# Small TensorE products padded with zeros to the full 128 rows and columns, in an audio tower on one core

## The chip, the cores and the metric

The kernel runs on one core of a Trainium2 chip. The metric is the device time of one execution in microseconds (us), lower is better. A core has five engines that run side by side, each through its own list of instructions in order: TensorE (PE in the profile, its weight loads apart as PEld), VectorE (DVE), ScalarE (ACT), GpSimd (POOL) and SyncE (SP, which here only issues DMAs). They wait for one another with semaphores.

TensorE multiplies a stationary operand (rows x columns, loaded by a LDWEIGHTS) with a moving operand that streams past it. The profile writes a product's form as `rows*columns` of the stationary operand, then `rows x columns` of the moving one: `16*128 16x121` has 16 rows of contraction, 128 stationary columns (rows of the result) and 121 moving columns. Each fp32 product leaves two MATMUL records, so x8 in a row of the trace is four products.

## The reference, cut to what matters

The input is 32 sequences of 80000 samples. Each is cut into 626 frames of 128 samples (zero-padded) and goes through a transform and four layers with residual sums, each behind a layer norm:

```python
h = frames(x) @ dct.T                                   # 626 tokens x 128
# 1: Mamba2, forwards and backwards: xBC = silu(conv4(u @ Win.T)), B and C are 16 columns each of it;
#    h_t = h_{t-1} * dA_t + dt_t * B_t x_t ;  y_t = C_t . h_t + D x_t ; gate, norm, projection
h = h + attn0(norm(h))
# 2: mixture of 8 experts, top 2: gelu(u @ w1 + b1) @ w2 + b2, weighed and summed
h = h + ffn0(norm(h))
# 3: attention over a window of 8 following tokens, per channel
h = h + attn1(norm(h))
# 4: gelu(u @ ip.T), top 64 of 512; gelu(. @ pw.T), top 128 of 256; softmax weights;
#    agg = weights @ process_values (64 columns); gelu(agg @ ow.T), top 64 of 512; @ op
h = h + ffn1(norm(h))
```

## The kernel before

One sequence is one block of work, and its four layers are four stages (`*_stage1` to `*_stage4`). Five tiles of 128 tokens make a sequence. The stages are pipelined over the sequences: in one iteration of the loop `Fori`, stage 1 works on sequence b, stage 2 on b-1, stage 3 on b-2 and stage 4 on b-3. With 32 sequences there are 35 iterations, the first three and the last three with fewer stages (written out), 29 full ones in between. In this text an iteration is cut at the first write of `h2` by VectorE (L1158) in one sequence and the next.

Each stage is written as a generator for each engine, and a string of digits (`PE_ORDER`, `ACT_ORDER`, `DVE_ORDER`, `POOL_ORDER`, `SP_ORDER`) says from which stage an engine takes its next piece. So each engine's order is fixed and mixes pieces of four stages; an engine that waits for one piece holds all pieces behind it.

What TensorE does, with the lines of the profile:

- Stage 1, projections (L566): 20 half units per sequence, each 4 products (the taps of the convolution) or 1 product (z) of 315 moving columns. Unit 0 of each direction makes B and C: its stationary operand has only `BC` = 48 columns (16 for B, a gap of 16, 16 for C), the result 48 rows. ScalarE applies silu and writes B to `Bw` and C to `Cs`, tiles of 16 rows.
- Stage 1, mixing: 12 chunks per sequence (6 chunks, 2 directions). For each, `mix(k)` makes the product C.B (L577, 16 rows of contraction, 121 moving columns) and two transposes of the inputs (L584); VectorE weighs the inputs (`Xw`, L1080) and the decays times C.B (`Mt`, L1083); `combine(k)` makes the skip products (L594) and four products of 64 stationary columns (L600); ScalarE copies the result (L863). Behind them stand the output products (L620) and row sums of 1 moving column (L628), for which VectorE waits at L1094.
- Stage 2, experts: MT = 17 tiles per sequence. `up(i)` has four products (L675), ScalarE applies gelu, and `down(i)` begins with the bias b2, added as a product of one row (a row of ones times b2, L684), then has four products (L686) and a transpose of a later tile (L663).
- Stage 4: for each of the 5 tiles transposes (L754), four products with 256 moving columns (L762), transposes (L772), the value product (L777, 64 stationary columns, so a result of 64 rows, copied to `aggT` by ScalarE, L992), the product with `owT` (L782, 64 rows of contraction, 512 moving columns), transposes (L791) and four products (L796), whose result VectorE adds at L1281.

VectorE's own work is above all the top-k selection of stage 4 (MAX8 and MATCH_REPLACE8, L1219, L1222, L1249, L1252), the scans of stage 1 (L1072) and the elementwise work of stage 3.

Of the kernel before, what the change touches and what calls it, by code (L numbers as in the profile page):

```python
# [13 lines left out]
P = 128  # L14
# [5 lines left out]
NS = 16  # L20
NH = 4
HD = 64
# [10 lines left out]
BC = 48  # L33
CW = 2 * P + BC
# [30 lines left out]
    ("ipT", NI), ("pwT", 4 * NP_), ("pv", 2 * HD), ("owT", NO), ("op", 4 * P),  # L65
# [72 lines left out]
def audio_tower(nc, NB, consts_d, setup_d, x_d, out_d, rows_d, experts_d, routed_d, answers_d):  # L138
    ctx = ExitStack()
    with ctx:  # L140
# [64 lines left out]
        Bw = [sb(f"Bw{d}", [NS, CH, P]) for d in range(2)]  # L205
        Cs = [sb(f"Cs{d}", [NS, CH, WIN]) for d in range(2)]
# [46 lines left out]
        aggT = sb("aggT", [HD, P])  # L253
# [23 lines left out]
        def weights_of(d, unit):  # L277

            if unit < 3:
                lo, n = ((2 * P, BC), (0, P), (P, P))[unit]  # L280
                return [(wconv[:, d, i, lo:lo + n], i) for i in range(TAPS)]
            z = c("wz").rearrange("p (d g n) -> p d g n", d=2, g=2)
            return [(z[:, d, unit - 3, :], TAPS - 1)]
# [10 lines left out]
        def b2_of(i):  # L294
            return expert[i % WR][0:1, 8 * P + KB:EC]
# [204 lines left out]
        def _(pool):  # L500
# [10 lines left out]
            for d in range(2):  # L511
                nc.gpsimd.memset(Bw[d][:, :, WIN:P], 0.0)
# [9 lines left out]
        def pe_stage1(pe, b):  # L522
# [27 lines left out]
            for n in range(HALF_UNITS):  # L550
                yield
                d, unit, half = n // 10, n % 10 // 2, n % 2
                yield
                if n == 2:
                    pe.wait_ge(G["dt_arg"].s, G["dt_arg"](b, 1))
                if n >= 3:
                    pe.wait_ge(G["proj_sb"].s, G["proj_sb"](b, n - 2))
                if n == DA_UNIT:

                    pe.wait_ge(G["dt_act"].s, G["dt_act"](b, 3))  # L560
                    at = 512 * (n % 3) + DA_AT
                    nc.tensor.transpose(pS[:, at:at + WIN], dtA_wide[:], ident[0:WIN, 0:WIN]).then_inc(G["dA_ps"].s, 1)
                blocks = weights_of(d, unit)
                rows = BC if unit == 0 else P
                for j, (wt, i) in enumerate(blocks):
                    last = nc.tensor.matmul(pS[0:rows, 512 * (n % 3):512 * (n % 3) + HQ], wt, tap(d, i, half * HQ, HQ),  # L566
                                            start=(j == 0), stop=(j == len(blocks) - 1))
                last.then_inc(G["proj_ps"].s, 1)
# [62 lines left out]
        def pe_stage2(pe, b):  # L631
# [47 lines left out]
            def down(i):  # L679
# [4 lines left out]
                nc.tensor.matmul(at, c("ones", 1), b2_of(i), start=True, stop=False)  # L684
# [53 lines left out]
        def pe_stage4(pe, b):  # L738
# [25 lines left out]
            for t in range(TILES):  # L764
# [11 lines left out]
                for j in range(2):  # L776
                    last = nc.tensor.matmul(pD[0:HD, 512:512 + P], c("pv")[:, j * HD:(j + 1) * HD], selT[:, j * P:(j + 1) * P],  # L777
# [4 lines left out]
                nc.tensor.matmul(pD[:, 0:NO], aggT[:], c("owT", HD), start=True, stop=True).then_inc(G["a3_ps"].s, 1)  # L782
# [30 lines left out]
        def act_stage1(act, b):  # L813
# [23 lines left out]
            for n in range(HALF_UNITS):  # L837
# [9 lines left out]
                if unit == 0:  # L847
                    nc.scalar.activation(Bw[d][:, half * CH // 2:(half + 1) * CH // 2, NS:WIN], px[0:NS].rearrange("p (c t) -> p c t", c=CH // 2),
                                         ACT.Silu, bias=cb[0:NS, d, 2:3])
                    last = nc.scalar.activation(Cs[d][:, half * CH // 2:(half + 1) * CH // 2, 0:Q], px[32:32 + NS].rearrange("p (c t) -> p c t", c=CH // 2),  # L850
# [108 lines left out]
        def act_stage4(act, b):  # L959
# [26 lines left out]
            for t in range(TILES):  # L986
# [5 lines left out]
                nc.scalar.copy(aggT[:], pD[0:HD, 512:512 + P]).then_inc(G["agg_sb"].s, 1)  # L992
# [9 lines left out]
        def _(act):  # L1002
# [4 lines left out]
            for d in range(2):  # L1007
                for ch in range(CH):
                    nc.scalar.copy(Bw[d][:, ch, 0:NS], ident[0:NS, 0:NS])
                    last = nc.scalar.copy(Cs[d][:, ch, Q:WIN], ident[0:NS, 0:NS])  # L1010
# [344 lines left out]
def laid_out(a):  # L1355
# [12 lines left out]
    def bc(x):  # L1368

        gap = np.zeros(x.shape[:-1] + (NS,), x.dtype)  # L1370
        return np.concatenate([x[..., 0:272], gap, x[..., 272:288]], -1)
# [20 lines left out]
    o["pv"] = a["L1_ffn_process_values"].reshape(2, P, HD).transpose(1, 0, 2)  # L1392
# [49 lines left out]
```

## Time and profile before

| | |
|---|---|
| device time, 3 runs | 8329.64 us median, 8313.04 to 8416.84 |
| profiled execution, span | 8631.7 us (what lies around the span is not shown; its time is at least this) |
| PE busy | 6340.7 us, 73% |
| DVE busy | 6951.3 us, 81% |
| ACT busy | 3240.6 us, 38% |
| POOL busy | 3053.8 us, 35% |
| mean granted TensorE clock | 0.752 of 2.4 GHz |

The busy time of an engine is the time in which it has an instruction at work. The clock granted to TensorE has two levels here, 1.00 (2.4 GHz) and 0.50 (1.2 GHz); 0.752 is their mean over the span. The profiled execution is 302 us longer than the median of the runs.

### The profile page before, as it was taken

The page shows a single profiled execution, that of the slowest core. Times are in us where ns is not written, and L with a number is a line of the kernel's source. Part 1 is how long each engine was busy: PE and PEld are TensorE (multiplying, and loading weights), DVE is VectorE, ACT ScalarE, POOL GpSimd, SP SyncE. Part 2 cuts the span into 40 slices and gives each one's busy share as a digit, 9 for nine tenths or more (in the row PEclk, how much of TensorE's full clock was granted, in tenths as well). Part 3 has the DMA queues.
Part 4 walks back from the last instruction along what each step waited for, and adds up shares of the span by engine and source line. Part 5 has one row for each costly group of instructions (what it writes and reads, how often), then busy time and mean ns, then how long its engine had stood idle before and what let it go on. Part 6 is the DMA issues. An engine that isn't in the chain of part 4 may idle for free.

```text
span 8631.7 us, 109592 instructions
## 1 busy us (share of the span) xinstructions
PE 6340.7 (73%) x31240; PEld 4768.2 (55%) x31240; DVE 6951.3 (81%) x22124; ACT 3240.6 (38%) x7204; POOL 3053.8 (35%) x3190
## 2 busy tenths in 40 slices
PE   6777778777777777777777777777777777777633
PEld 4555556555565555555555555555555555555422
DVE  2377978878888878889887979788879787889787
ACT  2343334433444433444443334433334433344311
POOL 2343433333333334333333433333333333333320
PEclk8887777776787767788776778777778777788655
DMA  2321222211222212222221222212222211222200
GB/s 68 103 79 52 61 79 75 69 55 54 69 79 75 65 47 67 69 80 76 74 63 50 61 78 77 72 57 59 59 79 76 71 58 55 62 80 76 62 6 3
DMA packets 342763, 561.43 MB, mean 65 GB/s; under 512 B 33728, under 2 KB 261792, under 8 KB 341664
## 3 DMA queue, kind: packets, MB, share of 16 engines
q10 hardware_dynamic: 152576, 357.68, 13.4%
q1 hardware_dynamic: 168992, 153.36, 6.8%
q0 software_dynamic: 20480, 41.98, 1.6%
q8 instruction: 311, 5.10, 0.3%
q14 instruction: 404, 3.31, 0.1%
HBM read 484.15 MB, written 68.74 MB: 64 GB/s over the span
## 4 chain that ended last, share of the span: by engine, by line
DVE 52%; PE 20%; issue 14%; DMA 4%; POOL 4%; ACT 3%; another core or an unknown queue 1%; ACTq 1%; SPq 1%; DVEq 0%; POOLq 0%
DVE m L1219 10%; DVE work L1252 7%; DVE work L1222 6%; DVE sorted L1249 6%; DVE a L1222 3%; PE pS L566 3%; DMA rows<-routed_rows 3%; DVE lg L1174 2%; DVE ab L1072 2%; PE pM L675 2%; PE pS L628 2%; PE pD L762 2%; PE pM L686 1%; POOL u L388 1%; DVE Mt L1083 1%
## 5 line engine op out<-in xcount | busy, mean ns | idle before, releaser
L1219 DVE MAX8 m<-work 128x8 f32<-128x512 f32 x1792 | 1144.6, 680 | 1.0
L1222 DVE MATCH_REPLACE8 work<-m,work 128x512 f32<-128x512 f32 x1536 | 1025.9, 675 | 0.0
L566 PE MATMUL pS<-u_fm,wconv_s 128*128 128x315 f32 (+1 forms) x3072 | 966.6, 470 | 0.2
L675 PE MATMUL pM<-turned,expert 128*128 128x128 f32 x4352 | 739.8, 323 | 244.2 <-ACT turned L921 243.2
L675 PEld LDWEIGHTS pM<-turned,expert 128*128 128x128 f32 x4352 | 660.9, 229 | 346.2 <-issue 328.6
L686 PE MATMUL pM<-expert,hid 128*128 128x128 f32 x4352 | 798.3, 340 | 0.0
L908 ACT ACTIVATE hid<-pM,expert 128x128 f32<-128x128 f32 x2176 | 619.4, 367 | 385.6 <-PE pM L675 383.8
L460 POOL TENSOR_TENSOR lg<-lg,red 128x640 f32<-128x640 f32 x256 | 388.2, 1553 | 996.5 <-DVE red L1180 996.5
L566 PEld LDWEIGHTS pS<-u_fm,wconv_s 128*128 128x128 f32 (+1 forms) x3072 | 526.6, 179 | 387.2 <-issue 154.7
L686 PEld LDWEIGHTS pM<-expert,hid 128*128 128x128 f32 x4352 | 674.6, 237 | 81.9 <-issue 35.1
L1252 DVE MATCH_REPLACE8 work<-sorted,work 128x128 f32<-128x128 f32 x2240 | 591.5, 276 | 0.0
L1219 DVE MAX8 m<-a 128x8 f32<-128x512 f32 x768 | 504.4, 677 | 71.7 <-issue 70.2
L1249 DVE MAX8 sorted<-work 128x8 f32<-128x128 f32 x2560 | 541.7, 279 | 1.1
L411 POOL TENSOR_TENSOR yg<-xs,zs 128x525 f32<-128x525 f32 (+1 forms) x256 | 198.0, 806 | 962.7 <-ACT xs L863 951.6
L999 ACT COPY selT<-pD 128x512 f32<-128x512 f32 x160 | 93.6, 585 | 1169.8 <-PE pD L791 1008.2
L1072 DVE TENSOR_TENSOR_SCAN ab<-ab,cst 121x488 f32<-121x488 f32 x384 | 489.8, 1282 | 36.7 <-DMA ab<-decay_rows 36.7
L489 POOL TENSOR_TENSOR lg<-lg 128x640 f32<-128x640 f32 x224 | 362.6, 1642 | 440.3 <-DVE lg L1185 435.3
L466 POOL TENSOR_TENSOR red<-lg 128x640 f32<-128x640 f32 x128 | 197.8, 1582 | 748.0 <-ACT lg L951 748.0
L921 ACT COPY turned<-pM 128x256 f32<-128x256 f32 (+1 forms) x544 | 196.7, 362 | 699.6 <-issue 356.2
L1080 DVE TENSOR_TENSOR Xw<-pS,dts 121x256 f32<-121x256 f32 x384 | 157.9, 411 | 367.2 <-PE pS L584 362.6
L600 PE MATMUL pS<-Mt,Xw 121*64 121x121 f32 x3072 | 311.9, 336 | 163.0 <-DVE Mt L1083 163.0
L796 PE MATMUL pD<-cst,selT 128*128 128x128 f32 x1280 | 294.4, 401 | 185.7 <-ACT selT L999 130.8
(242 smaller groups left out, 14472.6 us busy)
## 6 DMA issues: line engine op xcount, KB each, us to landing
expert<-in_experts ACTq DMA_DIRECT2D x544, 578.0 KB
ab<-decay_rows SPq DMA_DIRECT2D x384, 230.7 KB
rows<-routed_rows SPq DMA_DIRECT2D x128, 256.0 KB, 4.8
answer_rows<-turned ACTq DMA_DIRECT2D x256, 128.0 KB, 3.9
x_sb<-in_x SPq DMA_DIRECT2D x32, 256.0 KB
out<-hk SPq DMA_DIRECT2D x32, 256.0 KB
routed_rows<-un,slot POOLq DMA_INDIRECT x320
rows<-answer_rows,slot POOLq DMA_INDIRECT x320
```

The lines of the kernel that those rows point to most:

```text
L460: last = nc.gpsimd.tensor_tensor(lg[:, w, :], lg[:, w, :], red[:, 0, :], ALU.subtract)
L489: last = nc.gpsimd.tensor_tensor(lg[:, w, :], lg[:, w, :], lg[:, w + n, :], ALU.add)
L566: last = nc.tensor.matmul(pS[0:rows, 512 * (n % 3):512 * (n % 3) + HQ], wt, tap(d, i, half * HQ, HQ), start=(j == 0), stop=(j == len(block ...
L600: last = nc.tensor.matmul(pS[r * HD:(r + 1) * HD, B2 + g * WIN:B2 + (g + 1) * WIN], Xw[d][:, hh, :], Mt[d][:, hh, :], start=False, stop=(g ...
L675: last = nc.tensor.matmul(pM[:, bank(i) + j * P:bank(i) + (j + 1) * P], w1_of(i, j), turned[:, (i + 2) % 4, 1, :], start=True, stop=True)
L686: last = nc.tensor.matmul(at, hid[:, i % 2, j, :], w2_of(i, j), start=False, stop=(j == KB - 1))
L908: last = nc.scalar.activation(hid[:, i % 2, j, :], pM[:, at:at + P], ACT.Gelu, bias=b1_of(i, j))
L1072: nc.vector.tensor_tensor_scan(decays, decays, c("scan_src", WIN), 0.0, ALU.mult, ALU.add).then_inc(G["scanned"].s, 1)
L1219: link(nc.vector.max(m8[:, i, :], now[i]), len(tiles) - 1)
L1222: link(nc.vector.match_replace(work[i], m8[:, i, :], now[i], GONE), len(tiles) - 1)
L1249: link(nc.vector.max(top[:, 8 * r:8 * r + 8], left), 2 * n - 1)
L1252: link(nc.vector.match_replace(left, top[:, 8 * r:8 * r + 8], left, GONE), 2 * n - 1)
```

## The change

The products with few rows or columns are given zeros up to 128, and work on whole tiles:

- B and C projection: the stationary operand of unit 0 grows from 48 to 128 columns (`CW` from 304 to 384; the added columns of `wconv` and `convw` are zeros), the result from 48 to 128 rows. ScalarE still reads the same 32 rows of it.
- C.B: `Bw` and `Cs` grow from 16 to 128 rows, cleared once in the setup; the product has 128 rows of contraction.
- Expert bias: the row of ones becomes the whole 128x128 tile of ones, and b2 is read with all 128 rows, of which 127 are zeros already.
- Value product: `pv` gets 64 columns of zeros; the result has 128 rows, `aggT` 128 rows, and the product with `owT` 128 rows of contraction.

The number of instructions in the iterations and their order on every engine stay as they are. The four products of 64 columns at L600 stay as they are.

```diff
-BC = 48
-CW = 2 * P + BC
+CW = 3 * P
...
-    ("ipT", NI), ("pwT", 4 * NP_), ("pv", 2 * HD), ("owT", NO), ("op", 4 * P),
+    ("ipT", NI), ("pwT", 4 * NP_), ("pv", 2 * P), ("owT", NO), ("op", 4 * P),
...
-        Bw = [sb(f"Bw{d}", [NS, CH, P]) for d in range(2)]
-        Cs = [sb(f"Cs{d}", [NS, CH, WIN]) for d in range(2)]
+        Bw = [sb(f"Bw{d}", [P, CH, P]) for d in range(2)]
+        Cs = [sb(f"Cs{d}", [P, CH, WIN]) for d in range(2)]
...
-        aggT = sb("aggT", [HD, P])
+        aggT = sb("aggT", [P, P])
...
-                lo, n = ((2 * P, BC), (0, P), (P, P))[unit]
+                lo, n = ((2 * P, P), (0, P), (P, P))[unit]
...
-            return expert[i % WR][0:1, 8 * P + KB:EC]
+            return expert[i % WR][:, 8 * P + KB:EC]
...
-                nc.gpsimd.memset(Bw[d][:, :, WIN:P], 0.0)
+                nc.gpsimd.memset(Bw[d][:], 0.0)
+                nc.gpsimd.memset(Cs[d][:], 0.0)
...
-                rows = BC if unit == 0 else P
                 for j, (wt, i) in enumerate(blocks):
-                    last = nc.tensor.matmul(pS[0:rows, 512 * (n % 3):512 * (n % 3) + HQ], wt, tap(d, i, half * HQ, HQ),
+                    last = nc.tensor.matmul(pS[:, 512 * (n % 3):512 * (n % 3) + HQ], wt, tap(d, i, half * HQ, HQ),
...
-                nc.tensor.matmul(at, c("ones", 1), b2_of(i), start=True, stop=False)
+                nc.tensor.matmul(at, c("ones"), b2_of(i), start=True, stop=False)
...
-                    last = nc.tensor.matmul(pD[0:HD, 512:512 + P], c("pv")[:, j * HD:(j + 1) * HD], selT[:, j * P:(j + 1) * P],
+                    last = nc.tensor.matmul(pD[:, 512:512 + P], c("pv")[:, j * P:(j + 1) * P], selT[:, j * P:(j + 1) * P],
...
-                nc.tensor.matmul(pD[:, 0:NO], aggT[:], c("owT", HD), start=True, stop=True).then_inc(G["a3_ps"].s, 1)
+                nc.tensor.matmul(pD[:, 0:NO], aggT[:], c("owT"), start=True, stop=True).then_inc(G["a3_ps"].s, 1)
...
-                nc.scalar.copy(aggT[:], pD[0:HD, 512:512 + P]).then_inc(G["agg_sb"].s, 1)
+                nc.scalar.copy(aggT[:], pD[:, 512:512 + P]).then_inc(G["agg_sb"].s, 1)
```

ScalarE's writes to `Bw` and `Cs` name the first 16 rows now, and the host lays the zeros into `wconv`, `convw` and `pv`.

## Rows read from the trace of the kernel before

**Rows 1.** The page: span, chain of waits by engine, granted clock in 40 slices

```profile
span 8631.7 us, 109592 instructions
...
PEclk8887777776787767788776778777778777788655
...
DVE 52%; PE 20%; issue 14%; DMA 4%; POOL 4%; ACT 3%; another core or an unknown queue 1%; ACTq 1%; SPq 1%; DVEq 0%; POOLq 0%
...
```

**Rows 2.** Stretches: ramp-up and steady part, a row each

```profile
...
core 0: us, PE busy (x) PEld busy (x) DVE busy (x) ACT busy (x) POOL busy (x), PEclk, DMA share, GB/s
0.00:508.10 508.10, 362.86 (x2021) 277.30 (x2021) 152.55 (x408) 155.92 (x374) 169.36 (x207) 0.83 0.28 85
508.10:8017.80 7509.70, 5709.30 (x28304) 4310.36 (x28304) 6287.61 (x20039) 2954.26 (x6525) 2764.19 (x2871) 0.76 0.23 67
...
```

**Rows 3.** Stretches: the 13 long iterations, longest one and sum

```profile
...
5417.40:5690.40 273.00, 209.34 (x976) 157.97 (x976) 216.70 (x691) 101.95 (x225) 95.46 (x99) 0.72 0.21 64
...
sum 3495.50, PE 2689.25 PEld 2026.89 DVE 2824.20 ACT 1323.91 POOL 1239.46; mean PE 206.87 PEld 155.91 DVE 217.25 ACT 101.84 POOL 95.34
```

**Rows 4.** Stretches: the 16 short iterations, shortest one and sum

```profile
...
774.50:1019.10 244.60, 184.40 (x976) 138.67 (x976) 216.18 (x691) 101.75 (x225) 96.09 (x99) 0.81 0.24 71
...
sum 4014.20, PE 3020.05 PEld 2283.47 DVE 3463.40 ACT 1630.36 POOL 1524.72; mean PE 188.75 PEld 142.72 DVE 216.46 ACT 101.90 POOL 95.30
```

**Rows 5.** VectorE's waits in the long iteration 4381.2 to 4652.7

```profile
...
DVE Xw L1080 <- PE pS L584: 17.5, 5, 7.4
...
DVE vare L1094 <- PE pS L628: 5.5, 1, 5.5
DVE hk L1281 <- PE pD L796: 3.8, 2, 2.3
...
```

**Rows 6.** VectorE's waits in the short iteration 4132.7 to 4381.2

```profile
...
DVE Xw L1080 <- PE pS L584: 3.3, 2, 2.2
...
```

**Rows 7.** Stretches: 12 cold and busy ones, inside long iterations

```profile
...
4531.90:4600.10 68.20, 66.75 (x257) 47.60 (x257) 48.60 (x98) 17.28 (x55) 15.23 (x11) 0.50 0.23 65
...
sum 518.90, PE 508.88 PEld 365.65 DVE 342.54 ACT 126.66 POOL 124.32; mean PE 42.41 PEld 30.47 DVE 28.55 ACT 10.55 POOL 10.36
```

**Rows 8.** Stretches: a cold one without small products, and what follows it

```profile
...
4138.10:4142.70 4.60, 4.60 (x7) 1.63 (x6) 2.81 (x21) 1.56 (x3) 1.27 (x2) 0.50 0.00 2
4142.70:4152.90 10.20, 7.68 (x40) 4.75 (x39) 9.35 (x25) 5.18 (x12) 5.73 (x13) 1.00 0.00 0
...
```

**Rows 9.** TensorE in order of time, clock at 0.50, no idle time

```profile
...
4539.04 0.79 PE L684 MATMUL pM<-expert,cst 1*128 1x128 f32 x2
4539.76 2.08 PE L686 MATMUL pM<-expert,hid 128*128 128x128 f32 x8
4541.63 0.42 PE L663 MATMUL pM<-cst,rows 128*128 128x128 f32 x1
...
4543.82 2.07 PE L782 MATMUL pD<-cst,aggT 64*128 64x512 f32 x2
4545.83 0.78 PE L577 MATMUL pS<-Cs,Bw 16*128 16x121 f32 x2
4546.53 0.69 PE L584 MATMUL pS<-cst,xs 128*128 128x128 f32 x2
...
```

**Rows 10.** TensorE in order of time, clock at 1.00

```profile
...
4044.09 0.48 PE L684 MATMUL pM<-expert,cst 1*128 1x128 f32 x2
4044.50 1.16 PE L686 MATMUL pM<-expert,hid 128*128 128x128 f32 x8
4045.50 0.27 PE L663 MATMUL pM<-cst,rows 128*128 128x128 f32 x1
...
```

**Rows 11.** Weight loads of the projections, the two forms apart

```profile
...
L566 PEld LDWEIGHTS pS<-u_fm,wconv_s 128*128 128x128 f32 x2048 | 373.2, 190 | 162.2 <-issue 22.6 <-ACT Cs L850 9.8 <-DVE dtA L1063 5.0
...
L566 PEld LDWEIGHTS pS<-u_fm,wconv_s 128*48 128x48 f32 x1024 | 153.4, 157 | 225.0 <-issue 132.2 <-ACT zs L856 22.8
...
```

**Rows 12.** GpSimd in order of time, its longest memset of the setup

```profile
...
3.74 2.56 POOL L515 MEMSET xs<- 128x2968 f32 x1
...
```

More of the change, by code:

```diff
@@ L847, in act_stage1 @@
                 if unit == 0:
-                    nc.scalar.activation(Bw[d][:, half * CH // 2:(half + 1) * CH // 2, NS:WIN], px[0:NS].rearrange("p (c t) -> p c t", c=CH // 2),
+                    nc.scalar.activation(Bw[d][0:NS, half * CH // 2:(half + 1) * CH // 2, NS:WIN], px[0:NS].rearrange("p (c t) -> p c t", c=CH // 2),
                                          ACT.Silu, bias=cb[0:NS, d, 2:3])
-                    last = nc.scalar.activation(Cs[d][:, half * CH // 2:(half + 1) * CH // 2, 0:Q], px[32:32 + NS].rearrange("p (c t) -> p c t", c=CH // 2),
+                    last = nc.scalar.activation(Cs[d][0:NS, half * CH // 2:(half + 1) * CH // 2, 0:Q], px[32:32 + NS].rearrange("p (c t) -> p c t", c=CH // 2),
                                                 ACT.Silu, bias=cb[32:32 + NS, d, 2:3])
@@ L1008, in _ @@
                 for ch in range(CH):
-                    nc.scalar.copy(Bw[d][:, ch, 0:NS], ident[0:NS, 0:NS])
-                    last = nc.scalar.copy(Cs[d][:, ch, Q:WIN], ident[0:NS, 0:NS])
+                    nc.scalar.copy(Bw[d][0:NS, ch, 0:NS], ident[0:NS, 0:NS])
+                    last = nc.scalar.copy(Cs[d][0:NS, ch, Q:WIN], ident[0:NS, 0:NS])
             last.then_inc(a_exp, 1)
@@ L1370, in bc @@
         gap = np.zeros(x.shape[:-1] + (NS,), x.dtype)
-        return np.concatenate([x[..., 0:272], gap, x[..., 272:288]], -1)
+        return np.concatenate([x[..., 0:272], gap, x[..., 272:288], np.zeros(x.shape[:-1] + (P - 3 * NS,), x.dtype)], -1)
     o["wconv"] = np.concatenate([bc(x[256:544].T) for x in w], 1)
@@ L1391, in laid_out @@
     o["pwT"] = a["L1_ffn_process_input_weights"].T.reshape(4, P, NP_).transpose(1, 0, 2)
-    o["pv"] = a["L1_ffn_process_values"].reshape(2, P, HD).transpose(1, 0, 2)
+    pv = a["L1_ffn_process_values"].reshape(2, P, HD).transpose(1, 0, 2)
+    o["pv"] = np.concatenate([pv, np.zeros_like(pv)], -1)
     o["owT"] = a["L1_ffn_output_input_weights"].T
```

## The prediction, made before the changed kernel ran

> **What bounds the kernel now.** I read the page first. The chain of waits is 52% VectorE and 20% TensorE, and the granted clock moves between 0.5 and 0.8 or more in the slices [rows 1]. In the 7509.7 us of the 29 full iterations VectorE is busy 6287.6 us (84%) and TensorE 5709.3 us (76%) at a mean clock of 0.76; in the first 508.1 us TensorE is busy 362.9 us and VectorE 152.6 us [rows 2]. So VectorE bounds the steady part, and TensorE counts where VectorE waits for it. VectorE's 1222 us of idle time there is all that a faster TensorE could touch.
>
> Next I cut the steady part into its iterations, a row each. The work is the same in all (976 TensorE records), yet there are two kinds: 13 long ones, together 3495.5 us, 268.9 us each, up to 273.0 [rows 3], and 16 short ones, together 4014.2 us, 250.9 us each, down to 244.6 [rows 4]. VectorE's busy time is equal (217.3 and 216.5 us). TensorE's is 206.9 against 188.8 us, and its clock 0.70 to 0.74 against 0.77 to 0.81. The difference of 18.0 us is the clock's.
>
> VectorE's waits say where it lands. In a long iteration it waits 17.5 us at L1080 for the transposes of the mixing (L584), 5.5 us at L1094 and 3.8 us at L1281 [rows 5]; in a short one 3.3 us at L1080 [rows 6].
>
> Then I looked at TensorE just ahead of those waits. Twelve of the 13 long iterations hold one stretch of 34 to 68 us in which TensorE is busy nearly throughout and the clock stays at 0.50: 508.9 us busy of 518.9, VectorE busy 342.5 [rows 7]. The longest is 66.75 busy of 68.2 us. No short iteration has one over 17 us. In order of time such a stretch is the mixture of experts, chunks of the mixing and stage 4, with a bias product (L684, 1 row), a C.B product (L577, 16 rows) or an `owT` product (L782, 64 rows) every 2 to 3 us [rows 9]. Elsewhere a cold piece made of full products alone, 4.60 us of 4.60 busy, is followed by 10.2 us at 1.00 [rows 8]. So being busy doesn't bring the clock up in the first kind of stretch and does in the second, and what stands in the first and not in the second are products with few rows and the 64-column products of L600. The Trainium skill ("TensorE: Matmul & The Clock Gate", "What's actually happening") says that the gate goes by how busy TensorE has been; the 68 us stretch doesn't agree, unless few rows count for less, of which the page says nothing.
>
> **What the change does, part by part.**
>
> *Bias product, 17 per iteration.* Cold, it takes 0.72 us from its start to that of L686, while the four full products of the same width behind it take 1.87 us, 0.47 each [rows 9]. Warm it is 0.41 us against 1.00/4 = 0.25 [rows 10]. A padded bias product is in form exactly one of L686. It saves 0.25 us cold, 0.16 warm: 4.3 or 2.7 us per iteration. The Trainium skill says otherwise: in the same page, "Why this matters for your kernels", a product of 32 rows takes as long as one of 128, by which the saving would be 0. The rows show one of 1 row taking longer. The page "TensorEngine Tiling (Array Packing)", "Key Properties", gives a reason that agrees: a change of tiling mode drains TensorE.
>
> *C.B product, 12 per iteration.* 0.70 us cold [rows 9] against 0.47 for 128 moving columns: 0.23 saved, 2.8 us per iteration; warm, by the bias product's 0.16, 1.9 us. Its tiles are cleared once and their first 16 rows alone are rewritten, so nothing is added inside the loop.
>
> *`owT` product, 5 per iteration.* 2.01 us cold for 512 moving columns [rows 9], against 4 x 0.47 = 1.87: 0.14 saved, 0.7 us per iteration. ScalarE's copy to `aggT` has 128 rows in place of 64 and the same 128 elements per row; I take 0.
>
> *Value product, 10 per iteration, and B/C projection, 16 per iteration (four half units of 4).* These gain columns, not rows. The nearest row for a gain is the bias product's 0.25 us, for a loss the weight load: 157 ns for 48 columns against 190 ns for 128 [rows 11], 33 ns per record, two records per product. If it lay bare it would cost 32 x 0.033 = 1.1 us per iteration. The products of 315 columns beside it are far longer (by the 0.47 us for 128 columns cold, over 1 us), so they cover it. I take 0, the row of loads being nearer, and keep -2.5 and +1.1 us for the range.
>
> *Sum on TensorE.* 4.3 + 2.8 + 0.7 = 7.8 us per iteration cold, about 5 warm, some 6 in a short iteration.
>
> *What of it reaches the end.* In a short iteration VectorE waits 3.3 us for the mixing; with 6 us less ahead of it I take 2.5 of the 3.3, since part of TensorE's run begins only when VectorE has released it. 29 x 2.5 = 72 us. The bounds are 0, if the run always starts at VectorE's own release, and 3.3 x 29 = 96.
>
> *The clock.* If the small products are what holds the clock at 0.50, the cold stretches end within a few us, and the long iterations become short ones. All 13 would give 13 x 18.0 = 234 us. From the other side, 508.9 us of cold busy time run at twice the clock gives 254; the two agree. I take 11 of 13, since L600 keeps its 64 columns and some iterations will still fall badly: 198 us. The bounds are 0 and 234.
>
> *Ramp-up.* In 508.1 us TensorE is ahead of VectorE; about two iterations of small products, 2 x 6 = 12 us.
>
> *Setup.* Four memsets of 768 or 726 columns replace two tiny ones: 2988 columns at 2.56/2968 = 0.86 ns [rows 12] are 2.6 us, on the path, as TensorE, ScalarE and the zeroing DMA wait for `pool_setup`. With the larger constants +4 us. Nothing covers it, and it is paid once.
>
> The sum against the profiled execution is 198 + 72 + 12 - 4 = 278 us: its span would go from 8631.7 to about 8354, 3.2% less.
>
> **From the span to the median.** The median is 302 us under that span, more than the 234 us of all 13 long iterations. Either the profiler costs time, or the runs have fewer long iterations; their spread of 104 us is 6 of them. If they have few, there is less to win. I take two thirds of the clock's term, 130 us: 8330 - 130 - 72 - 12 + 4 = **8120 us**.
>
> **Rivals.**
>
> *A: only the switches are saved.* The runs have hardly a long iteration, or the padded zeros don't lift the clock. By the skill's rule that the gate goes by busy time it would be so too. What is left is 72 + 12 - 4 = 80: 8250 us, 8200 to 8300. For it speaks the median, which is near an execution of short iterations alone (8631.7 - 234 = 8398, and lower); against it the 12 stretches.
>
> *B: it doesn't do what it says, for time.* A product of 128 rows of zeros costs what one of 1 row does, and the 0.72 us were the wait for hid or the bank: about 8335. Against it: C.B, with other tiles and other waits, shows the same 0.70.
>
> *C: slower.* TensorE gets through its work sooner, so it idles longer before each release by VectorE; the clock falls in these gaps, and each run then begins at 0.50. The place is the mixing and L620 to L628, and it shows in the short iterations becoming long: 16 x 18.0 = 288 us, less the 80: 8540 us. It decides against the change once more than 5 of the 16 turn (80/18 = 4.4) with none of the long ones cured. For it speaks that TensorE idles 62 us in a short iteration already; against it that the short iterations, which idle no less, are the warm ones.
>
> **How the numbers follow.** Forecast 0.62, A 0.27, B 0.05, C 0.06. The low end is both terms whole and half of the value product's bound (2.5 x 32 = 80), 8330 - 234 - 96 - 40 = 7960; the high end reaches through A to 8270. Two per cent, about what a measurement of this kernel can tell from no change, is 8163. The forecast case lies under it but for a few hundredths, and A's lower end hardly reaches it: faster 0.61, same 0.33, slower 0.06.
>
> **What the profile after would show.** Right: a mean clock of 0.80 or more; no cold, busy stretch over 20 us; nearly all iterations at 245 to 252 us; the bias product at 0.47 or 0.25 us; VectorE's wait at L1080 (L1079 there) at 4 us or less in nearly every iteration. VectorE's waits at L1094 and L1281 stay, as the products ahead of them were full before. Wrong: long iterations still about a dozen (the clock isn't held by the small products), or the switch time still at the padded products.

## The result, and the profile after

| | before | after |
|---|---|---|
| device time, median | 8339.6 us (8313.04 to 8416.84, 4 runs) | 8142.81 us (8130.81 to 8145.41, 4 runs) |
| ratio, 95% interval | | 0.9727 (0.9667 to 0.9787) |
| profiled execution, time and span | 8631.7 us span | 8142.98 us, span 8141.2 us |

The kernel is 2.7% faster by the ratio, an estimate of its own with its interval, and 2.4% by the quotient of the two medians (0.9764). Its runs also lie within 14.6 us of one another, those of before within 104 us. Ratios are taken over undisturbed runs alone, while a median may stand over all of them, so the two can differ by some tenths of a per cent below too.

The page of the changed kernel, its lines that answer to [rows 1], with the busy time of the engines ahead of them:

```profile
span 8141.2 us, 109594 instructions
...
PE 5529.4 (68%) x31240; PEld 4441.6 (55%) x31240; DVE 6959.1 (85%) x22124; ACT 3232.6 (40%) x7204; POOL 3040.7 (37%) x3192
...
PEclk8887788878788888788877788878788878778755
...
DVE 67%; PE 9%; issue 8%; DMA 5%; POOL 5%; ACT 3%; ACTq 2%; SPq 1%; DVEq 0%; POOLq 0%
```

The mean clock went from 0.752 to 0.800, and VectorE's share of the chain from 52 to 67%: VectorE is still at work 6959 us, and waits less. Next the stretches of the changed kernel, cut as in [rows 2 to 4]: the ramp-up, the longest iteration, then the sum of all 29 full iterations.

```profile
...
core 0: us, PE busy (x) PEld busy (x) DVE busy (x) ACT busy (x) POOL busy (x), PEclk, DMA share, GB/s
0.00:491.40 491.40, 332.92 (x2021) 273.49 (x2021) 154.37 (x408) 155.51 (x374) 173.59 (x209) 0.85 0.29 89
...
3646.80:3891.80 245.00, 173.48 (x976) 139.44 (x976) 216.80 (x692) 101.79 (x226) 94.68 (x99) 0.80 0.25 71
```

```profile
...
sum 7045.80, PE 4961.00 PEld 4004.98 DVE 6293.62 ACT 2946.70 POOL 2746.90; mean PE 171.07 PEld 138.10 DVE 217.02 ACT 101.61 POOL 94.72
```

There is one kind of iteration left: 240.9 to 245.0 us, 243.0 in the mean, with TensorE busy 171.1 us in each against 206.9 and 188.8 [rows 3, 4]. No stretch of 17 us or more is busy throughout at 0.50 any longer. Before, there were twelve of 34 us and more by [rows 7], and a thirteenth that the prediction overlooked, in the one long iteration that it took for an exception (1019.1 to 1281.9). So every long iteration has one:

```profile
...
1169.70:1214.10 44.40, 43.00 (x168) 30.93 (x168) 26.09 (x44) 11.84 (x38) 13.29 (x8) 0.50 0.28 83
```

The waits of VectorE over the whole execution (total, times, longest):

```profile
...
DVE work L1240 <- ACT a L970: 239.9, 30, 8.7
...
DVE Xw L1079 <- PE pS L583: 158.5, 103, 20.6
...
DVE hk L1280 <- PE pD L795: 57.8, 35, 4.0
DVE vare L1093 <- PE pS L627: 50.5, 3, 17.8
```

The wait for the mixing (L1079, L1080 before) is 158.5 us in 103 places, ramp-up and end included. The 29 full iterations alone, 491.4 to 7537.2, have less than half of it:

```profile
...
DVE Xw L1079 <- PE pS L583: 64.8, 87, 2.6
```

That is 2.2 us per iteration, 3.8 in the worst; in one long iteration of before it was 17.5 us, in a short one 3.3 [rows 5, 6]. TensorE in order of time, first at 1.00, then at 0.50, to be read beside [rows 10] and [rows 9]:

```profile
...
2031.92 0.39 PE L683 MATMUL pM<-expert,cst 128*128 128x128 f32 x2
2032.15 1.06 PE L685 MATMUL pM<-expert,hid 128*128 128x128 f32 x8
2033.04 0.27 PE L662 MATMUL pM<-cst,rows 128*128 128x128 f32 x1
```

```profile
...
2069.41 0.64 PE L683 MATMUL pM<-expert,cst 128*128 128x128 f32 x2
2069.84 1.92 PE L685 MATMUL pM<-expert,hid 128*128 128x128 f32 x8
2071.55 0.42 PE L662 MATMUL pM<-cst,rows 128*128 128x128 f32 x1
```

From start to start the bias product (L683) takes 2032.15 - 2031.92 = 0.23 us warm, where it was 0.41, and 2069.84 - 2069.41 = 0.43 us cold, where it was 0.72. A product of L685 takes (2033.04 - 2032.15)/4 = 0.22 warm and (2071.55 - 2069.84)/4 = 0.43 cold. The padded product is a full one, and costs what a full one costs. The four products of L685 became quicker too, though nothing in them was changed: 0.89 us warm against 1.00 [rows 10], 1.71 cold against 1.87 [rows 9]. From the bias product to the transpose of L662 it is 1.12 us against 1.41 warm and 2.14 against 2.59 cold. So one tile saves 0.29 and 0.45 us, where the prediction had 0.16 and 0.25.

**A difference that isn't the change's.** The profiled execution of before had a span of 8631.7 us, 302 over the median beside it. The runs below were made on three chips, and the unchanged kernel takes 8330.58 us on one of them, 8617.28 and 8620.74 on the two others. By its level that trace comes from a chip like the latter two, the times and the trace of after from one like the former; the waits of ScalarE shown further down say the same. So each kernel below is compared with the unchanged one on its own chip, and "the quicker chip" and "the slower chip" are said where it matters. Of e1, e2, e3 and e5 below the whole interval lies under 1, but the ratio is less than 2% away from it.

### The profile page after: what moved, and what is told of

The parts are those of the page before. It is cut to its first block, busy times and chain, and to the rows that moved or that the text cites. A ratio compares the mean times of both kernels' runs of the same rounds, so it can differ in the third digit from the quotient of the medians.

```text
span 8141.2 us, 109594 instructions
## 1 busy us (share of the span) xinstructions
PE 5529.4 (68%) x31240; PEld 4441.6 (55%) x31240; DVE 6959.1 (85%) x22124; ACT 3232.6 (40%) x7204; POOL 3040.7 (37%) x3192
## 3 DMA queue, kind: packets, MB, share of 16 engines
q10 hardware_dynamic: 152576, 357.68, 14.2%
## 4 chain that ended last, share of the span: by engine, by line
DVE 67%; PE 9%; issue 8%; DMA 5%; POOL 5%; ACT 3%; ACTq 2%; SPq 1%; DVEq 0%; POOLq 0%
DVE m L1218 15%; DVE work L1221 9%; DVE work L1251 7%; DVE sorted L1248 6%; DVE a L1221 4%; DVE ab L1071 3%; DMA rows<-routed_rows 3%; DVE lg L1173 2%; PE pS L565 2%; PE pD L761 2%; DVE Mt L1082 2%; DMA decay_rows<-dAT 2%; POOL u L387 2%; DVE stats L1030 2%; DVE red L1188 2%
## 5 line engine op out<-in xcount | busy, mean ns | idle before, releaser
L565 PE MATMUL pS<-u_fm,wconv_s 128*128 128x315 f32 x3072 | 929.0, 457 | 6.1 <-ACT Cs L849 5.8
L674 PE MATMUL pM<-turned,expert 128*128 128x128 f32 x4352 | 655.2, 297 | 331.7 <-ACT turned L920 327.4
L674 PEld LDWEIGHTS pM<-turned,expert 128*128 128x128 f32 x4352 | 586.0, 206 | 423.6 <-issue 359.9
L565 PEld LDWEIGHTS pS<-u_fm,wconv_s 128*128 128x128 f32 x3072 | 614.2, 205 | 256.3 <-issue 52.8
L685 PE MATMUL pM<-expert,hid 128*128 128x128 f32 x4352 | 672.9, 306 | 0.0
L685 PEld LDWEIGHTS pM<-expert,hid 128*128 128x128 f32 x4352 | 631.6, 223 | 0.0
L599 PE MATMUL pS<-Mt,Xw 121*64 121x121 f32 x3072 | 294.2, 321 | 488.7 <-DVE Mt L1082 486.4
L599 PEld LDWEIGHTS pS<-Mt,Xw 121*64 121x64 f32 x3072 | 189.2, 160 | 585.7 <-DVE Mt L1082 532.9
L382 POOL TENSOR_TENSOR rstd<-vare,mhalf 128x5 f32<-128x5 f32 x160 | 187.1, 1170 | 624.8 <-DVE vare L1036 624.8
```

What stands on the lines that cost most here:

```text
L565: last = nc.tensor.matmul(pS[:, 512 * (n % 3):512 * (n % 3) + HQ], wt, tap(d, i, half * HQ, HQ), start=(j == 0), stop=(j == len(blocks) - 1))
L599: last = nc.tensor.matmul(pS[r * HD:(r + 1) * HD, B2 + g * WIN:B2 + (g + 1) * WIN], Xw[d][:, hh, :], Mt[d][:, hh, :], start=False, stop=(g ...
L674: last = nc.tensor.matmul(pM[:, bank(i) + j * P:bank(i) + (j + 1) * P], w1_of(i, j), turned[:, (i + 2) % 4, 1, :], start=True, stop=True)
L685: last = nc.tensor.matmul(at, hid[:, i % 2, j, :], w2_of(i, j), start=False, stop=(j == KB - 1))
```

## The experiments

### One part of the change at a time, on the quicker chip

The unchanged kernel took 8330.58 us there (median of 19, 8235.92 to 8726.48).

`e1_bias_only`: the expert bias alone is padded.

```diff
-            return expert[i % WR][0:1, 8 * P + KB:EC]
+            return expert[i % WR][:, 8 * P + KB:EC]
...
-                nc.tensor.matmul(at, c("ones", 1), b2_of(i), start=True, stop=False)
+                nc.tensor.matmul(at, c("ones"), b2_of(i), start=True, stop=False)
```

> The kernel before with the bias product alone padded to 128 rows. Clock theory (products with few rows hold TensorE's clock at 0.50 though TensorE is busy): the bias stands in every cold stretch, so most of them end early; time 8180 to 8240 us, mean clock 0.77 or more, hardly an iteration over 262 us. Switch theory (only the time of changing the tiling mode is saved, 0.16 to 0.25 us a product, little of it where VectorE waits): 8290 to 8320 us, and the long iterations as many as in the kernel before. In both, a bias product takes 0.47 us cold and 0.25 us warm.

Measured: 8176.82 us, ratio 0.9871 (0.9802 to 0.9939), a little under the range of the clock theory. No iteration is over 245.6 us. The padded product takes 0.22 us warm, where 0.25 was expected.

`e2_cb_only`: the C.B product alone, with 128 rows of contraction.

```diff
-        Bw = [sb(f"Bw{d}", [NS, CH, P]) for d in range(2)]
-        Cs = [sb(f"Cs{d}", [NS, CH, WIN]) for d in range(2)]
+        Bw = [sb(f"Bw{d}", [P, CH, P]) for d in range(2)]
+        Cs = [sb(f"Cs{d}", [P, CH, WIN]) for d in range(2)]
...
```

The rest of this edit clears both tiles in the setup and lets ScalarE write their first 16 rows.

> The kernel before with C.B alone padded from 16 to 128 rows. Clock theory: it cures part of the cold stretches, 8210 to 8280 us. Switch theory: its 12 products stand right ahead of the transposes for which VectorE waits, 0.16 to 0.23 us each, so at most 2.5 us an iteration, 8260 to 8320 us, with long iterations left. This one tells the two apart by the iterations of the profile more than by the time.

Measured: 8214.36 us, ratio 0.9896 (0.9861 to 0.9931); no iteration over 246.1 us.

`e3_value_only`: the value product gets its 64 columns of zeros and the product with `owT` its 128 rows.

```diff
-                    last = nc.tensor.matmul(pD[0:HD, 512:512 + P], c("pv")[:, j * HD:(j + 1) * HD], selT[:, j * P:(j + 1) * P],
+                    last = nc.tensor.matmul(pD[:, 512:512 + P], c("pv")[:, j * P:(j + 1) * P], selT[:, j * P:(j + 1) * P],
...
-                nc.tensor.matmul(pD[:, 0:NO], aggT[:], c("owT", HD), start=True, stop=True).then_inc(G["a3_ps"].s, 1)
+                nc.tensor.matmul(pD[:, 0:NO], aggT[:], c("owT"), start=True, stop=True).then_inc(G["a3_ps"].s, 1)
...
```

> The kernel before with the value product (64 to 128 columns) and the product with owT (64 to 128 rows) alone padded. Clock theory: the owT product is the widest of the small ones (512 moving columns, 2.0 us cold), so fewer or shorter cold stretches, 8230 to 8300 us. Switch theory: 5 x 0.14 us an iteration, 8310 to 8340 us, the same as before.

Measured: 8177.55 us, ratio 0.9872 (0.9803 to 0.9941), more than either theory had said; no iteration over 246.3 us. Its 29 full iterations:

```profile
...
sum 7051.30, PE 5367.29 PEld 4100.40 DVE 6267.86 ACT 2951.10 POOL 2778.18; mean PE 185.08 PEld 141.39 DVE 216.13 ACT 101.76 POOL 95.80
```

They take 7051.3 us, the changed kernel's 7045.8, though TensorE is busy 185.1 us in each here and 171.1 there. So 14 us less work of TensorE per iteration are worth 0.2 us per iteration: in the full iterations the time of the small products themselves hardly reaches the end. In the ramp-up, where TensorE is ahead of VectorE, it does: the first 512.7 us of e3 are the first 491.4 of the changed kernel.

`e4_proj_only`: the B and C projection alone, 48 to 128 stationary columns.

```diff
-                lo, n = ((2 * P, BC), (0, P), (P, P))[unit]
+                lo, n = ((2 * P, P), (0, P), (P, P))[unit]
...
```

> The kernel before with the B and C projection alone padded from 48 to 128 columns. Both theories: no product has more rows, and the pitch of the 315-column products is set by the moving columns, so 8320 to 8360 us, the same as before. If the columns of the stationary operand counted for the clock too, it would be faster, 8200 to 8300 us. If the longer weight load (190 ns against 157) lay bare, slower by 1.1 us an iteration, 35 us.

Measured: 8311.18 us, ratio 0.9988 (0.994 to 1.0036), no change. Its profiled execution took 8338.82 us, as much as the 8339.6 of the kernel before. Its sums of the 11 long iterations and of the 18 short ones, then two of its cold and busy stretches, the longest one among them, and its wait for the mixing, over the whole execution and in the full iterations:

```profile
...
sum 2850.30, PE 2248.42 PEld 1722.97 DVE 2383.68 ACT 1119.40 POOL 1049.84; mean PE 204.40 PEld 156.63 DVE 216.70 ACT 101.76 POOL 95.44
```

```profile
...
sum 4374.00, PE 3334.41 PEld 2586.31 DVE 3890.12 ACT 1828.71 POOL 1720.30; mean PE 185.24 PEld 143.68 DVE 216.12 ACT 101.60 POOL 95.57
```

```profile
...
1394.20:1455.60 61.40, 59.84 (x233) 42.65 (x234) 41.24 (x77) 17.52 (x52) 15.88 (x9) 0.50 0.26 74
2629.80:2698.10 68.30, 66.81 (x257) 47.67 (x259) 48.70 (x98) 17.39 (x57) 15.35 (x11) 0.50 0.22 65
```

```profile
...
DVE Xw L1078 <- PE pS L582: 348.3, 111, 24.0
```

```profile
...
DVE Xw L1078 <- PE pS L582: 235.6, 94, 7.4
```

This kernel is in effect the kernel before, profiled on the quicker chip, which is what my working had lacked. Long iterations are 259.1 us, short ones 243.0, which is the changed kernel's mean. VectorE is equally busy in both, TensorE 204.4 against 185.2 us. The stretches at 0.50 are there in full length, 66.81 us busy of 68.3: eleven of 34 us or more, one in each long iteration and none in a short one. The wait for the mixing in a short iteration is 2.9 us in the mean, in a long one 16.7.

What follows from the four: three of the parts end the long iterations, each by itself: rows are added to 17, 12 or 5 products per iteration; the fourth, which pads columns of one product and no row of contraction, ends none.

### Rows, or the drain of the engine? On the slower chip

The unchanged kernel took 8617.28 us there (median of 7, 8598.0 to 8654.92). The question was whether the long iterations go because TensorE no longer stops between products of different form, or because more rows are at work.

`e7_bias_64_rows`: the bias product gets 64 rows, 63 of them zeros.

```diff
-            return expert[i % WR][0:1, 8 * P + KB:EC]
+            return expert[i % WR][0:64, 8 * P + KB:EC]
...
-                nc.tensor.matmul(at, c("ones", 1), b2_of(i), start=True, stop=False)
+                nc.tensor.matmul(at, c("ones", 64), b2_of(i), start=True, stop=False)
```

> The kernel before with the bias product at 64 rows in place of 1 (rows 1 to 63 of b2 are zeros). If the time lies in the switching and the product stays in a split mode at 64 rows, a product still takes 0.41 us warm and 0.72 cold. Clock theory with rows counting one by one: half of what 128 rows add, so most long iterations go, 8180 to 8260 us. Switch theory, or a clock that asks only for the full mode: as before, 8310 to 8350 us.

Measured: 8379.08 us, ratio 0.9717 (0.9682 to 0.9752). TensorE in order of time at 1.00, to be read beside [rows 10], the sum of the 29 iterations, and one of the longest stretches that are still cold and busy, 13.7 us:

```profile
...
2089.02 0.49 PE L684 MATMUL pM<-expert,cst 64*128 64x128 f32 x2
2089.43 1.16 PE L686 MATMUL pM<-expert,hid 128*128 128x128 f32 x8
2090.43 0.27 PE L663 MATMUL pM<-cst,rows 128*128 128x128 f32 x1
```

```profile
...
sum 7292.20, PE 5491.84 PEld 4160.27 DVE 6287.94 ACT 2956.61 POOL 2765.80; mean PE 189.37 PEld 143.46 DVE 216.83 ACT 101.95 POOL 95.37
```

```profile
...
4919.00:4932.70 13.70, 13.52 (x64) 10.57 (x65) 9.76 (x22) 5.36 (x20) 0.88 (x1) 0.50 0.46 118
```

The bias product takes 2089.43 - 2089.02 = 0.41 us, to the hundredth what it took with one row, the four products behind it 1.00 us as in [rows 10], and TensorE is busy 189.4 us per iteration, more than in a short one of before [rows 4]. So nothing was saved on the products, and yet no iteration is over 258.9 us and 2.8% of the time is gone. The products take the same time as before, so what ended the cold stretches isn't a change in TensorE's own timing. The Trainium skill ("TensorE: Matmul & The Clock Gate", "Why this matters for your kernels") has a product of 32 rows take as long as one of 128. This trace doesn't agree: 64 rows and 1 row cost the same here, 0.41 us, and 128 cost 0.18 us less.

`e6_zeros_added`: the bias product stays as it was, and a full product of a zeroed tile is added behind each one.

```diff
                 nc.tensor.matmul(at, c("ones", 1), b2_of(i), start=True, stop=False)
+                nc.tensor.matmul(at, c("ones"), none[:], start=False, stop=False)
...
```

> The kernel before, and behind each 1-row bias product one more full product of 128 rows that adds zeros (17 an iteration). All small products and their switches stay, and TensorE has 17 x 0.25 to 0.47 us more to do. Clock theory: more work and yet faster, since the clock comes up: 8190 to 8260 us, no long iterations. Switch theory: 4 to 8 us more for TensorE in each iteration, some of it where VectorE waits: 8340 to 8450 us.

Measured: 8461.67 us, ratio 0.9814 (0.9777 to 0.9852). TensorE in order of time at 0.50:

```profile
...
2161.05 0.79 PE L686 MATMUL pM<-expert,cst 1*128 1x128 f32 x2
2161.77 0.80 PE L687 MATMUL pM<-none,cst 128*128 128x128 f32 x2
2162.36 1.49 PE L689 MATMUL pM<-expert,hid 128*128 128x128 f32 x6
```

The one-row product keeps its 0.72 us, as in [rows 9], and a full one comes on top, 17 times per iteration. That one takes 2162.36 - 2161.77 = 0.59 us where a full one takes 0.43: the product behind a one-row product pays as well. The kernel has more work on TensorE and is 1.9% quicker. No iteration is over 260.6 us. Ten cold and busy stretches are left, but of 20.5 us each, 205 us together.

`e9_owt_rows_only`: only the product with `owT` gets 128 rows, 5 products per iteration; the value product keeps its 64 columns.

```diff
-        aggT = sb("aggT", [HD, P])
+        aggT = sb("aggT", [P, P])
...
+            nc.gpsimd.memset(aggT[:], 0.0)
...
-                nc.tensor.matmul(pD[:, 0:NO], aggT[:], c("owT", HD), start=True, stop=True).then_inc(G["a3_ps"].s, 1)
+                nc.tensor.matmul(pD[:, 0:NO], aggT[:], c("owT"), start=True, stop=True).then_inc(G["a3_ps"].s, 1)
...
-                nc.scalar.copy(aggT[:], pD[0:HD, 512:512 + P]).then_inc(G["agg_sb"].s, 1)
+                nc.scalar.copy(aggT[0:HD], pD[0:HD, 512:512 + P]).then_inc(G["agg_sb"].s, 1)
```

> The kernel before with five products an iteration changed: the product with owT has 128 rows of contraction in place of 64 (the added rows of aggT are cleared once); the value product keeps 64 columns. Clock theory: the rows are what counts, so this alone gives what padding value product and owT gave together, 8170 to 8190 us, with no iteration over 262 us. Switch theory: 5 x 0.14 us an iteration, 20 us at most, 8310 to 8340 us with long iterations left.

Measured: 8391.36 us, ratio 0.9741 (0.9697 to 0.9785); no iteration over 256.9 us. Its wait for the mixing:

```profile
...
DVE Xw L1081 <- PE pS L585: 212.8, 88, 28.5
```

Rows in five products per iteration end the long iterations; the value product's columns aren't needed for it.

`e5_all_but_bias`: the whole change without the bias.

```diff
-                nc.tensor.matmul(at, c("ones"), b2_of(i), start=True, stop=False)
+                nc.tensor.matmul(at, c("ones", 1), b2_of(i), start=True, stop=False)
...
```

> The changed kernel with the bias product back at 1 row. Clock theory: each part alone took the long iterations away, so taking one part back brings none: 8150 to 8180 us. Switch theory: the bias products are the most numerous, so half of the gain goes, 8220 to 8260 us.

Measured: 8495.16 us, ratio 0.9861 (0.9823 to 0.99). The long iterations are gone here too (250.9 to 256.9 us), but it is slower than e7 and e9 on the same chip, each of which does less. That was a miss, and asked for a look at the slower chip itself.

### What the slower chip does otherwise

These four ran on the third chip, the other one of the slower kind. The unchanged kernel took 8620.74 us there (median of 7, 8586.42 to 8679.01).

`e10_before_again` is the kernel before, and `e11_after_again` the changed one, both without any edit, to have the two traces from one chip.

> The kernel before, unchanged, for a trace from the same chip as the three runs beside it. The levels of two chips differed by some 280 us for it (8331 and 8617 us), while the share of its time that an edit saves was alike. Clock theory: 8 or more of the 29 full iterations are long (over 255 us) with a cold and busy stretch in each, and the short ones are as long as those of the changed kernel on this chip, within 3 us. Switch theory: all iterations are longer by some us, the short ones too.

> The changed kernel on the chip of the run before it. Both theories: 2 to 3.5% less than the kernel before. Clock theory: no cold and busy stretch over 25 us.

Measured: e10 8603.93 us with a span of 8602.1, so the profile adds nothing that shows. e11 8452.18 us, ratio 0.9787 (0.9727 to 0.9847), so whether it is 2% is open. e10 has ten iterations of 261.4 to 271.7 us, each with a cold and busy stretch of 34 us or more, and 19 of at most 258.9 us without one, 251.9 in the mean. e11 has no stretch of 17 us or more, and all its iterations lie between 245.4 and 257.0 us, but at 254.4 in the mean. So here the short iterations became 2.5 us longer. What was expected of e10 missed in its last part: its 13 iterations under 255 us are 249.8 in the mean, 4.6 under those of e11. The waits over the whole execution, of all engines, first e10, then e11:

```profile
...
DVE Xw L1080 <- PE pS L584: 339.4, 114, 29.1
...
ACT selT L999 <- remote: 149.1, 18, 9.4
...
DVE vare L1094 <- PE pS L628: 140.5, 26, 18.4
...
DVE hk L1281 <- PE pD L796: 112.3, 51, 4.1
```

```profile
...
ACT selT L998 <- remote: 231.8, 27, 9.7
...
DVE vare L1093 <- PE pS L627: 183.0, 30, 18.7
...
DVE Xw L1079 <- PE pS L583: 157.8, 103, 21.2
...
DVE hk L1280 <- PE pD L795: 141.9, 62, 4.1
```

The wait for the mixing falls by 339.4 - 157.8 = 182 us, as on the quicker chip (348.3 in e4, 158.5 in the changed kernel). But VectorE's waits at L1093 and L1280 (L1094 and L1281 before) grow by 183.0 + 141.9 - 140.5 - 112.3 = 72 us, and ScalarE's copy of `selT` waits 27 times, 8.6 us in the mean, for something for which the profile names no releaser (it calls it "remote"). VectorE's own waits at the two lines have some such entries too; with all entries counted they grow by 54 us. In the five traces from the quicker kind of chip (after, e1 to e4) the copy has no such wait. The trace of before has it, as e10 does:

```profile
...
ACT selT L999 <- remote: 151.7, 18, 9.3
...
```

TensorE around one of them, first e11, then the same place of the changed kernel on the quicker chip:

```profile
...
2991.37 0.66 PE L790 MATMUL pD<-cst,a 128*128 128x128 f32 x4 [0.78 <-issue]
...
2991.86 0.60 PE L722 MATMUL pA<-cst,kf 128*128 128x128 f32 x4
2998.20 2.08 PE L795 MATMUL pD<-cst,selT 128*128 128x128 f32 x8 [5.74 <-ACT selT L998]
3000.07 8.53 PE L627 MATMUL pS<-cst,zs 128*128 128x1 f32 x40
```

```profile
...
2893.99 0.60 PE L722 MATMUL pA<-cst,kf 128*128 128x128 f32 x4
2894.83 1.16 PE L795 MATMUL pD<-cst,selT 128*128 128x128 f32 x8 [0.24 <-ACT selT L998]
2895.83 4.73 PE L627 MATMUL pS<-cst,zs 128*128 128x1 f32 x40
```

The transposes of L790 that the copy reads had ended at 2992.03, but it began at 2997.56 only. TensorE idles 5.74 us for that copy, the granted clock falls to 0.50 in the gap, and the 40 row sums behind it (L627), for which VectorE waits, take 8.53 us in place of 4.73. In places like this one a part of the gain is given back on this chip.

`e12_small_added`: the changed kernel with a one-row product of zeros put back behind each padded bias product. If the stops of the engine counted, it would lose what the change won.

```diff
                 nc.tensor.matmul(at, c("ones"), b2_of(i), start=True, stop=False)
+                nc.tensor.matmul(at, c("ones", 1), none[0:1, :], start=False, stop=False)
...
```

> The changed kernel, and behind each padded bias product one more product of a single row that adds zeros: 17 switches into a split mode and back come back in each iteration, 0.41 us warm and 0.72 us cold each, 7 to 12 us of TensorE's time, and nothing is taken from the padded ones. Clock theory: the switches' time lies beside VectorE's work, so within 0.6% of the changed kernel, and no long iterations. Switch theory: most of the gain is lost, 1.5% or more over the changed kernel.

Measured: 8361.2 us, ratio 0.9691 (0.9632 to 0.975): with more work it is 1.1% quicker than the changed kernel on the same chip, against what I expected. Its waits:

```profile
...
DVE Xw L1082 <- PE pS L585: 178.4, 84, 22.3
...
DVE vare L1096 <- PE pS L629: 113.4, 25, 19.6
...
DVE hk L1283 <- PE pD L798: 80.1, 41, 4.2
...
ACT selT L1001 <- remote: 73.6, 10, 8.9
```

The wait for the mixing is nearly as in e11, those at L1096 and L1283 are 131 us shorter (183.0 + 141.9 - 113.4 - 80.1; 123 with the entries of other releasers counted), and the copy of `selT` waits 10 times for the unnamed releaser in place of 27.

`e13_l600_padded`: bias, C.B and value product padded, the projection not, and the products of L600 made with 128 stationary columns, half of them zeros.

```diff
-                    last = nc.tensor.matmul(pS[r * HD:(r + 1) * HD, B2 + g * WIN:B2 + (g + 1) * WIN], Xw[d][:, hh, :], Mt[d][:, hh, :],
-                                            start=False, stop=(g == 1))
+                    last = nc.tensor.matmul(pS[:, B2 + g * WIN:B2 + (g + 1) * WIN], Xw[d][:, (2 * hh - r) * HD:(2 * hh - r + 2) * HD], Mt[d][:, hh, :],
+                                            start=False, stop=(hh == NH - 1))
...
```

> The changed kernel with the B and C projection back at 48 columns, and the four products of each chunk (64 stationary columns in pairs side by side) at 128 columns, half of them zeros: they no longer run in pairs. Clock theory: these are the last narrow products, so the clock rises once more (0.81 or more), but each chunk takes 1.0 us warm in place of 0.6 and 1.87 cold in place of 1.0; TensorE has slack, so the time stays within 1% of the changed kernel's. Switch theory: 12 x 0.4 us and more an iteration for TensorE right ahead of VectorE's waits, so slower than the changed kernel by 1% or more.

Measured: 8460.68 us, ratio 0.9802 (0.9745 to 0.9859), as much as e11. The copy of `selT` waits 29 times there, 247.0 us together. The mean clock rose to 0.795 (e11 0.781), less than the 0.81 expected, and nothing came of it.

## Why the prediction was right, and where it was not

**Forecast 8120, measured 8143.** The saving was 210 us in the prediction and 196.8 measured, so the sum fits; its terms fit less well, and that the sum fits is in part luck. e4, the kernel before but for columns of zeros in one product, gives the account on the quicker chip. Its span is 8337.0 - 8141.2 = 195.8 us over the changed kernel's.

| term | predicted for the median | measured, e4 against after |
|---|---|---|
| clock, long iterations become short | 130 (whole 234) | 11 x 16.1 = 177 |
| switch time in short iterations | 29 x 2.5 = 72 | 18 x 0.0 = 0 |
| ramp-up | 12 | 506.9 - 491.4 = 15.5 |
| tail | not named | 605.8 - 604.0 = 2 |
| setup | -4 | not seen, inside the ramp-up |
| sum | 210 | 195 |

**The clock term: right, and cut too far.** The mechanism is the one forecast: the cold, busy stretches are gone, on the quicker chip all iterations are of the short kind, e1, e2, e3 and e9 show it part by part, and e7 and e6 show it with nothing saved on TensorE's products. The 11 and the 16.1 us are near the 13 and the 18.0 worked out from [rows 3, 4]. I then took two thirds of the 198 for a reason that doesn't hold (below). Left at 198 the term would have been nearer to its 177, and the sum farther off, at 8052.

**The switch term: wrong.** "In a short iteration VectorE waits 3.3 us for the mixing; with 6 us less ahead of it I take 2.5 of the 3.3" is the step that failed. TensorE's work did shrink, by 14.2 us per iteration against e4's short ones, more than twice the 6 of the prediction. The padded products cost 0.23 and 0.43 us against 0.25 and 0.47 forecast, and the products behind them became quicker as well, which the sum on TensorE left out; the clock was also a hundredth or so higher. But the wait for the mixing fell only from 2.9 us in e4's short iterations to 2.2, not by 2.5 us, and the iteration stayed at 243.0 us. This is the lower bound given there, 0, "if the run always starts at VectorE's own release". e3 against after says it a second time, 0.2 us per iteration for 14 us of TensorE.

**From the span to the median: wrong reasons.** Neither does the profiler cost time (8603.93 us for a span of 8602.1 in e10, 8142.98 for 8141.2 in after), nor have the runs fewer long iterations (11 in e4 at a median near before's). The chip was another one. The errors of this step and of the switch term, -47 and +72 us, offset each other in good part, and 8120 owes its closeness to that luck. On the kind of chip from which the rows came the sum did worse: 278 us were forecast between the two spans, and e10 and e11 are 8602.1 - 8471.9 = 130 apart. The 29 iterations give 86 of it: about 134 by the ten long ones, less 48 by the other 19, which became longer. The ramp-up gives 35.

**Projection and value product at 0.** For the projection that is right: e4 gives 0.9988. For the value product's columns no run shows them apart; e9 ends the long iterations without them.

**Rival A (only the switches are saved) is refuted as it stood**: it kept the switch term and dropped the clock, and the runs did the reverse. e7 keeps every switch and wins 2.8%; e12 puts 17 one-row products per iteration back and loses nothing. What is more, in the 29 full iterations the wait for the mixing falls by 235.6 - 64.8 = 171 us between e4 and the changed kernel, nearly all of the 178.5 us by which they get shorter. The rule of the Trainium skill on which it leant ("TensorE: Matmul & The Clock Gate", "What's actually happening": the gate goes by how busy the engine is) doesn't describe the stretch of 68.3 us in e4, 66.81 of it busy, at 0.50 throughout.

**Rival B** is refuted by the timeline of after, 0.43 us where it was 0.72. **Rival C** named a real effect, TensorE idle, the clock down, the next run cold, and placed it at L620 to L628. It didn't decide the sign: on the slower chip VectorE's waits at L1093 and L1280 took back 72 us of 182 (54 with all entries counted), and the short iterations grew by 2.5 us but didn't turn long. Why the copy ahead of them is late is not shown. That those two waits "stay" was right on the quicker chip (57.4 and 58.8 us in e4, 50.5 and 57.8 after) and wrong on the slower one.

**The signs given beforehand.** Clock 0.80 and no cold, busy stretch over 20 us: as said. Iterations at 245 to 252 us: 240.9 to 245.0, the same gain on a quicker chip. L1079 at 4 us or less: 3.8 at most, as said, but with 2.9 before it in a short iteration that sign told little.

**What stays open.** Why the same kernel takes 3.4% longer on some chips; what releases ScalarE's copy of `selT` there; and why its waits come 27 and 29 times in e11 and e13, 10 to 13 times in e12, e9, e7 and e6, and 18 in e10. The number goes with the time that was given back (e5, at 27, is the slow one of its group), which says where the time went in these single traces and not why. By the ratios the whole change (0.9787, 27 waits) gained less on a slower chip than e7 (0.9717) and e9 (0.9741) did with one part each on the other. That the mix of small and full products shifts when this copy falls is a guess that no run tested. Open too is what in the rows holds the clock: 64 rows in the bias product help, though `owT` with 64 rows was part of the cold stretches, and no experiment shows a law behind that. Nor was the order of the pieces or their timing ever shifted apart from rows and products, to see whether the stretches end by that too; e7, in which rows alone are added and no time changes, speaks against it.

## What to carry to other kernels

When iterations of equal work come in two lengths, cut them apart and read the granted clock in stretches in which TensorE is busy throughout: a stretch that is full and still at 0.50, with products of few rows in it, is worth trying a padding with zeros (five products per iteration gave 2.6% here). Try the parts one by one: on the slower chips the whole change gave less than one part. Don't count the same products' own time as a gain before the trace shows that the engine behind them waits for their end; 14 us of TensorE per full iteration bought none. And set a trace only against times from its own chip: compare the profiled execution's time with the median first, and where they differ by more than the runs do, read the mechanism from the trace and the size from neither.

## What the runs showed of the hardware that was not expected

- With products of 1, 16 and 64 rows among full ones, stretches up to 68.3 us, 98% busy, stayed at 0.50, and more rows of zeros ended them: 64 to 128 rows in 5 products per iteration gave 0.9741, 1 to 64 rows in 17 products 0.9717, the latter without any change in TensorE's own time. 48 to 128 stationary columns in the projection changed nothing (0.9988). Columns may still count elsewhere: with L600 at 128 columns (e13, its projection not padded) the mean clock was 0.795 against the 0.781 of e11.
- A full product of zeros *added* behind each one-row product made the kernel quicker, 0.9814.
- A product of 128 moving columns with 1 or 64 rows, between full ones, takes 0.41 us warm (0.72 cold, one row), a full one 0.23 (0.43). The Trainium skill ("TensorEngine Tiling (Array Packing)", "Key Properties") has a change of tiling mode drain the engine, which agrees with that. The full products behind one are slower too (four of them 1.00 us against 0.89 warm, 1.87 against 1.71 cold), so if that is the reason, going there and back costs some 0.29 us warm and 0.45 cold here.
- Three chips ran the unchanged kernel at 8330.58, 8617.28 and 8620.74 us, 3.4% apart, and in the traces at the slower level alone one copy of ScalarE has waits without a named releaser, 6 to 9 us in the mean of a trace.
